# Another order of steps in the second half of a transformer block, on one core

## The chip, the core and the metric

The kernel is one program on one core of a Trainium2 chip. The metric is the device time of one execution in microseconds (us); the median of three runs is the figure that the change is judged by. A core has five engines that run their own instruction lists side by side: TensorE (PE in the rows), VectorE (DVE), ScalarE (ACT), GpSimd (POOL) and SyncE (SP, which here only issues DMAs). They meet by counting semaphores.

## The reference, cut to what matters

```python
x = x + attention(layernorm(x))          # x: 8 batches x 1024 tokens x 256, float32
x = x + ffn(layernorm(x))

# ffn, per token; n = layernorm(x)
gf = global_net(mean over the batch's tokens of n)      # one number for each batch
out = n
for cycle in range(3):
    h = gelu(out @ w1 + b1)      # 256 -> 256
    h = gelu(h @ w2 + b2)        # 256 -> 128
    h = gelu(h @ w3 + b3)        # 128 -> 64
    tf = sigmoid(h @ w4 + b4)    # one number for each token
    coupling = 0.1 + range * ((0.7 * gf + 0.3 * tf) - 0.5) * 2
    out = out + coupling * twist(out)    # twist swaps and negates quarters of the row
```

Since twist applied twice is minus the identity, `out` is always a * n + b * twist(n) with two numbers a, b for each token. So the kernel multiplies n by w1 and by its twisted form once, and each cycle only mixes the two products.

## The kernel before

The first half (attention_phase) ends at about 525 us; the change doesn't touch it. The second half (ffn_phase) treats the 8192 tokens as 16 groups of 512 (NGROUPS, numbered m below; two make a batch). For one group the steps are, with the line that does the main work:

- **stats** (DVE L215 to L221, then the power -1/2 on POOL, L228): mean and 1/sqrt(variance).
- **scale** (DVE L236, four instructions): x0 = normalised tokens.
- **turn** 0, 1 (PE L1272, eight transposes): x0 into PSUM; ACT L1073 copies it (x0T_hi), DVE L1154 makes the rest x0T_lo.
- **product** 0 to 3 (PE L1288 to L1290, six matmuls each): the two products, two chunks of each; ACT L1081 copies each to SBUF (made).
- **global** 0 to 2 (PE L1302, L1307, L1311 with an ACT step behind each, DVE L1160): once in a batch, at its second group.
- Then three cycles c = 0, 1, 2: **spread** c (c = 1, 2; PE L1331: the a and b of the tokens are spread over partitions), **mix** c (DVE L1172, for c = 2 L1169 too, multiply; POOL L1050 adds), **gelu1** c (ACT L1108), **h2** c (PE L1342, ACT L1115), **h3** c (PE L1350 and L1354, ACT L1122), **dot** c (POOL L1057 multiplies by w4, DVE L1180 adds up), **squash** c (ACT L1131 tanh, then small DVE instructions L1222 to L1256 that make the coupling and the new a, b).
- **final** 0 to 3 (DVE L1193, L1201, L1204 each): the result, stored by SP (L1024).

The groups are pipelined. The dictionary PERIODS holds for each engine an order written out by hand: in period n it takes the steps ("kind", ahead, ...) one after the other, each for group m = n + ahead. An engine never changes that order, so a step that waits holds everything behind it on that engine. walk_periods goes through the periods; the first ones and the last ones are written out, the middle is a loop of two turns over four periods (SLOTS). In a period four groups are in flight: one is turned and has its products, and cycles 0, 1 and 2 run on it and the two or three groups before it. In the trace a period is the stretch from one L1272 to the next.

Of the kernel before, what the change touches and what calls it, by code (L numbers as in the profile page):

```python
# [260 lines left out]
def attention_phase(nc, f, x, wqkv, wo, cos_t, sin_t, w, x2):  # L261
# [4 lines left out]
    with ExitStack() as ctx:  # L266
# [606 lines left out]

PERIODS = {
    "tensor": [
        ("product", -1, 0), ("global", -1, 2), ("product", -1, 1), ("spread", -2, 1),
        ("spread", -3, 2), ("product", -1, 2), ("h2", -1, 0), ("product", -1, 3), ("h3", -1, 0),
        ("h2", -2, 1), ("h2", -3, 2), ("turn", 0, 0), ("turn", 0, 1), ("h3", -2, 1),
        ("global", 0, 0), ("h3", -3, 2), ("global", 0, 1),
    ],  # L880
    "scalar": [
        ("product", -1, 3), ("h3", -1, 0), ("h2", -2, 1), ("h2", -3, 2), ("turn", 0, 0),
        ("turn", 0, 1), ("global", 0, 0), ("h3", -2, 1), ("h3", -3, 2), ("global", 0, 1),
        ("squash", -2, 1), ("squash", -1, 0), ("global", 0, 2), ("squash", -3, 2),
        ("product", 0, 0), ("product", 0, 1), ("gelu1", 0, 0), ("h2", 0, 0), ("gelu1", -1, 1),
        ("product", 0, 2), ("gelu1", -2, 2),
    ],
    "vector": [
        ("scale", 0), ("stats", 1), ("turn", 0, 0), ("turn", 0, 1), ("dot", -2, 1), ("dot", -1, 0),
        ("dot", -3, 2), ("squash", -2, 1), ("global", 0, 2), ("squash", -1, 0), ("squash", -3, 2),  # L890
        ("mix", -1, 1), ("mix", -2, 2), ("final", -3, 0), ("final", -3, 1), ("final", -3, 2),
        ("final", -3, 3),
    ],
    "gpsimd": [
        ("dot", -1, 0), ("stats", 1), ("dot", -2, 1), ("dot", -3, 2), ("mix", -1, 1),
        ("mix", -2, 2),
    ],
}
AHEAD = max(step[1] for steps in PERIODS.values() for step in steps)
# [505 lines left out]
```

How the kernel before makes its waits and increments, by code:

```python
def at_least(engine, semaphore, value):  # L39
    if isinstance(value, int) and value <= 0:
        return
    engine.wait_ge(semaphore, value)
# [167 lines left out]
def ffn_moments(dve, f, m, slot, x_tiles):  # L211
    at_least(dve, f.moments_ready, m * G)
    for t in range(G):
        dve.bn_stats(f.stats[:, t, :], x_tiles[t])
    dve.drain()
    for t in range(G):
        dve.bn_aggr(f.moments[slot][:, t, :], f.stats[:, t, :]).then_inc(f.moments_ready, 1)
    dve.wait_ge(f.moments_ready, m * G + G)
    dve.tensor_scalar(f.var_eps[slot][:], f.moments[slot][:, :, 1], EPS, None,
                      ALU.add).then_inc(f.var_ready, 1)
# [2 lines left out]
def ffn_rstd(pool, f, m, slot):  # L225
    pool.wait_ge(f.var_ready, m + 1)
    pool.tensor_tensor(f.rstd[slot][:], f.var_eps[slot][:], f.minus_half[:].to_broadcast([P, G]),
                       ALU.pow).then_inc(f.rstd_ready, 1)
# [2 lines left out]
def ffn_scale(dve, f, m, slot, x0, x_tiles):  # L232
    dve.wait_ge(f.rstd_ready, m + 1)
    for t in range(G):
        dve.tensor_scalar(x0[:, t, :], x_tiles[t], f.moments[slot][:, t, 0:1],
                          f.rstd[slot][:, t:t + 1], ALU.subtract, ALU.mult).then_inc(f.x0_ready, 1)
# [154 lines left out]
        @block.sync  # L392
# [13 lines left out]
            sp.wait_ge(zeroed, 8)
            with nc.allow_non_contiguous_dma(reason="small vectors"):
# [3 lines left out]
            def store_and_load(b, turn, n):  # L413
# [1 line left out]
                for g in range(GROUPS):  # L415
                    sp.wait_ge(x2_ready, b * TILES + G * (g + 1))
                    sp.dma_start(x2_view[b, :, tiles(g), :],
```

## Time and profile before

| | us |
|---|---|
| median of 3 runs | 928.47 |
| the three runs | 931.96, 926.84, 928.47 |
| profiled execution, its span | 926.4 |
| second half in it | 525.7 to 926.4 |
| TensorE busy | 814.3 |
| VectorE busy | 720.2 |
| ScalarE busy | 464.4 |
| GpSimd busy | 363.7 |

The span of the profiled execution is the time from its first to its last instruction. The page gives no figure of its own for what lies around it; the span is 2.1 us under the median of the runs and 0.4 us under the fastest of them. The granted clock is a share of TensorE's full 2.4 GHz; a stretch at 0.5 ran at 1.2 GHz, a stretch between was partly at either level.

### The profile page before, as it was taken

Reading aid. Unit: us, or ns where it says so; the run is one execution under the profiler, and the core shown is the slowest. Engines: PE = TensorE matmul, PEld = TensorE weight load, DVE = VectorE, ACT = ScalarE, POOL = GpSimd, SP = SyncE. Lnnn points to the kernel's source line nnn. Section 1 sums busy time; section 2 is a strip of 40 time slices with the busy share of each in tenths; the row PEclk is TensorE's granted clock in tenths of the full one; section 3 lists DMA queues with packets and bytes.
Section 4 is the critical chain, followed back from the end, with each engine's and each line's share of the span. In section 5 each row is a group of like instructions: output and inputs, shape, how many; then the busy total and the mean of one; then the engine's idle time right before and its main releaser. Section 6 shows DMA issues by size and latency. Waiting matters only on the chain. (4 is left out here: it accounts for less than half of the span.)

```text
span 926.4 us, 15342 instructions
## 1 busy us (share of the span) xinstructions
PE 814.3 (88%) x4368; PEld 644.3 (70%) x4368; DVE 720.2 (78%) x1567; ACT 464.4 (50%) x1020; POOL 363.7 (39%) x377
## 2 busy tenths in 40 slices
PE   4689999998999989999999789988879889999952
PEld 3578788887888868888888557666656666666731
DVE  6779898896998978989978736777777878776575
ACT  2355565554565645565555255444444445444421
POOL 4535644364256434642460014333333334333331
PEclk9889999999999999999999899877897989877865
DMA  6000011101110110011000250000000100000011
GB/s 186 1 1 29 19 46 47 46 1 50 46 36 12 47 49 24 24 47 46 2 0 2 81 192 1 23 24 23 19 28 0 41 27 24 24 24 23 11 35 45
DMA packets 34588, 32.60 MB, mean 35 GB/s; under 512 B 3524, under 2 KB 34244, under 8 KB 34500
## 3 DMA queue, kind: packets, MB, share of 16 engines
q1 hardware_dynamic: 34500, 31.56, 10.7%
q8 instruction: 39, 0.64, 0.3%
q14 instruction: 49, 0.40, 0.1%
HBM read 16.88 MB, written 14.68 MB: 34 GB/s over the span
## 5 line engine op out<-in xcount | busy, mean ns | idle before, releaser
L507 ACT ACTIVATE pT_hi<-bank 128x512 fp32r<-128x512 f32 x192 | 90.9, 492 | 104.6 <-PE bank L843 96.1
L554 ACT ACTIVATE x_all<-scores_ps,neg_max 128x384 f32<-128x384 f32 (+7 forms) x128 | 94.6, 739 | 46.3 <-DVE neg_max L684 42.4
L580 DVE TENSOR_TENSOR pT_lo<-bank,pT_hi 128x512 fp32r<-128x512 f32 x192 | 100.7, 547 | 21.3 <-ACT pT_hi L507 21.3
L684 DVE TENSOR_REDUCE neg_max<-scores_ps 128x1 f32<-128x384 f32 (+7 forms) x128 | 95.3, 749 | 23.9 <-PE scores_ps L816 17.9
L843 PE MATMUL bank<-ident,x_all 128*128 128x128 f32 x576 | 92.7, 279 | 22.3 <-DVE pT_lo L580 17.3
L384 POOL TENSOR_TENSOR rope_a<-x_all,cos_sb 128x384 f32<-128x384 f32 x60 | 61.7, 1028 | 116.7 <-ACT x_all L507 112.6
L1342 PE MATMUL cycle_ps<-h,w_sb 128*128 128x512 f32 x192 | 92.3, 617 | 12.0 <-ACT h L1108 12.0
L843 PEld LDWEIGHTS bank<-ident,x_all 128*128 128x128 f32 x576 | 66.6, 142 | 35.4 <-DVE pT_lo L580 22.3
L1057 POOL TENSOR_TENSOR h_w<-h,w_sb 128x256 f32<-128x256 f32 x48 | 35.6, 742 | 113.1 <-ACT h L1122 113.1
L731 PE MATMUL oT_ps<-pT_hi,v_hi 128*128 128x512 f32 x192 | 77.3, 402 | 0.5 <-DVE oT_lo L580 0.4
L731 PE MATMUL scores_ps<-k_hi,q_hi 128*128 128x512 f32 (+1 forms) x192 | 71.6, 373 | 0.0
L1288 PE MATMUL made_ps<-x0T_hi,w_hi 128*128 128x512 f32 x128 | 68.9, 538 | 2.7 <-DVE x0T_lo L1154 2.7
L1050 POOL TENSOR_TENSOR mixed<-part_b,made 128x1024 f32<-128x1024 f32 x16 | 38.0, 2378 | 81.4 <-DVE part_b L1172 81.4
L1342 PEld LDWEIGHTS cycle_ps<-h,w_sb 128*128 128x128 f32 x192 | 36.0, 196 | 46.6 <-issue 27.4
L732 PE MATMUL oT_ps<-pT_lo,v_hi 128*128 128x512 f32 x192 | 67.0, 349 | 0.0
L497 POOL TENSOR_TENSOR rot<-rope_a,rope_b 128x384 f32<-128x384 f32 x64 | 66.2, 1034 | 1.9 <-DVE rope_a L384 1.8
L733 PE MATMUL oT_ps<-pT_hi,v_lo 128*128 128x512 f32 x192 | 66.9, 348 | 0.0
L483 POOL TENSOR_TENSOR rope_b<-x_all,sin_sb 128x384 f32<-128x384 f32 x64 | 66.4, 1037 | 1.3 <-ACT x_all L507 0.8
L733 PE MATMUL scores_ps<-k_hi,q_lo 128*128 128x512 f32 (+1 forms) x192 | 66.8, 348 | 0.0
L1354 PE MATMUL cycle_ps<-w_sb,h 128*128 128x64 f32 x384 | 66.7, 329 | 0.0
L732 PE MATMUL scores_ps<-k_lo,q_hi 128*128 128x512 f32 (+1 forms) x192 | 66.4, 346 | 0.0
L1354 PEld LDWEIGHTS cycle_ps<-w_sb,h 128*128 128x128 f32 x384 | 59.2, 235 | 7.6 <-issue 3.4
(132 smaller groups left out, 2120.3 us busy)
## 6 DMA issues: line engine op xcount, KB each, us to landing
x_all<-x SPq DMA_DIRECT2D x16, 512.0 KB, 3.6
out<-x_all SPq DMA_DIRECT2D x16, 512.0 KB, 3.0
x<-x_all SPq DMA_DIRECT2D x12, 512.0 KB, 3.0
x_all<-x SPq DMA_DIRECT2D x6, 1024.0 KB, 5.9
x_all<-wqkv SPq DMA_DIRECT2D x1, 512.0 KB, 4.6
sin_sb<-sin_t SPq DMA_DIRECT2D x1, 512.0 KB, 7.0
cos_sb<-cos_t SPq DMA_DIRECT2D x1, 256.0 KB, 5.8
x_all<-wo SPq DMA_DIRECT2D x1, 256.0 KB, 5.9
```

The costliest lines, as they stand in the source:

```text
L483: pool.tensor_tensor(rope_b[:].rearrange("p (c e d) -> p c e d", e=2, d=HALF), qk[:, :, ::-1, :], sin.rearrange("p c (e d) -> p c e d", e= ...
L507: return nc.scalar.activation(out, in_, ACT.Copy)
L554: nc.scalar.activation(probs[u % 2][:, k, 0:keys], scores_ps[k % 2][:, 0:keys], ACT.Exp, bias=neg_max[:, u * G + k:u * G + k + 1], accum_o ...
L580: return dve.tensor_tensor(out, whole, hi.bitcast(F32), ALU.subtract)
L684: dve.tensor_reduce(neg_max[:, u * G + k:u * G + k + 1], scores_ps[k % 2][:, 0:keys], AX_X, ALU.max, negate=True).then_inc(max_ready, 1)
L731: nc.tensor.matmul(out, stationary[0], moving[0], start=first, stop=False)
L732: nc.tensor.matmul(out, stationary[0], moving[1], start=False, stop=False)
L733: return nc.tensor.matmul(out, stationary[1], moving[0], start=False, stop=last)
L843: mm = nc.tensor.transpose(ps[:, k * P:(k + 1) * P], probs[u % 2][:, k, j * P:(j + 1) * P], ident[:])
L1288: nc.tensor.matmul(ps[:], hi, x0T_hi[:, k, :], start=k == 0, stop=False)
L1342: mm = nc.tensor.matmul(cycle_ps[c][:], f.w2_sb[:, k, :], h1[c][:, k, :], start=k == 0, stop=k == DC - 1)
L1354: mm = nc.tensor.matmul(ps[:, t * H3:(t + 1) * H3], h2[c][:, t * P:(t + 1) * P], f.w3_sb[:], start=False, stop=t == G - 1)
```

## The change

Only the four lists of PERIODS are replaced. The steps and what each computes are the same, and so are all waits. Much of the difference in the numbers "ahead" is a renumbering: where all entries of an engine's list are shifted together, its list of instructions stays the same but for the place where the loop closes. What is left, with "T" for the group that is turned in the period, is this.

- PE before: turn T, h3 1, global 0, h3 2, global 1, product 0, global 2, product 1, spread 1, spread 2, product 2, h2 0, product 3, h3 0, h2 1, h2 2. After: turn T, h3 0, global 0, h3 2, global 1, global 2, product 0, spread 1, spread 2, products 1 to 3, h2 0, h2 1, h2 2, h3 1.
- DVE before: turn, dots 1, 0, 2, squashes 1, 0, 2, mix 1, mix 2, finals, scale T+1, stats T+2. After: turn, dots 1, 0, squashes 0, 1, mix 1, mix 2, dot 2, squash 2, finals, scale T+1, stats T+2.
- ACT before: squash 2 ahead of product 0's copy; the copy of product 3 ahead of h3 0. After: squash 2 behind products 0, 1 and gelu1 0; the copy of product 3 behind the turn and h3 0; h2 1 ahead of h2 0.
- POOL before: the power for stats T+2's group between dot 0 and dot 1, ahead of the mixes. After: behind both mixes.

```diff
 PERIODS = {
     "tensor": [
-        ("product", -1, 0), ("global", -1, 2), ("product", -1, 1), ("spread", -2, 1),
-        ("spread", -3, 2), ("product", -1, 2), ("h2", -1, 0), ("product", -1, 3), ("h3", -1, 0),
-        ("h2", -2, 1), ("h2", -3, 2), ("turn", 0, 0), ("turn", 0, 1), ("h3", -2, 1),
-        ("global", 0, 0), ("h3", -3, 2), ("global", 0, 1),
+        ("product", 0, 0), ("spread", -1, 1), ("spread", -2, 2), ("product", 0, 1),
+        ("product", 0, 2), ("product", 0, 3), ("h2", 0, 0), ("h2", -1, 1), ("h2", -2, 2),
+        ("h3", -1, 1), ("turn", 1, 0), ("turn", 1, 1), ("h3", 0, 0), ("global", 1, 0),
+        ("h3", -2, 2), ("global", 1, 1), ("global", 1, 2),
     ],
     "scalar": [
-        ("product", -1, 3), ("h3", -1, 0), ("h2", -2, 1), ("h2", -3, 2), ("turn", 0, 0),
-        ("turn", 0, 1), ("global", 0, 0), ("h3", -2, 1), ("h3", -3, 2), ("global", 0, 1),
-        ("squash", -2, 1), ("squash", -1, 0), ("global", 0, 2), ("squash", -3, 2),
-        ("product", 0, 0), ("product", 0, 1), ("gelu1", 0, 0), ("h2", 0, 0), ("gelu1", -1, 1),
-        ("product", 0, 2), ("gelu1", -2, 2),
+        ("global", 0, 2), ("squash", -1, 0), ("h3", -3, 2), ("product", 0, 0), ("product", 0, 1),
+        ("gelu1", 0, 0), ("squash", -3, 2), ("product", 0, 2), ("gelu1", -1, 1), ("gelu1", -2, 2),
+        ("h2", -1, 1), ("h2", 0, 0), ("h2", -2, 2), ("h3", -1, 1), ("turn", 1, 0), ("turn", 1, 1),
+        ("h3", 0, 0), ("product", 0, 3), ("global", 1, 0), ("global", 1, 1), ("squash", -1, 1),
     ],
     "vector": [
-        ("scale", 0), ("stats", 1), ("turn", 0, 0), ("turn", 0, 1), ("dot", -2, 1), ("dot", -1, 0),
-        ("dot", -3, 2), ("squash", -2, 1), ("global", 0, 2), ("squash", -1, 0), ("squash", -3, 2),
-        ("mix", -1, 1), ("mix", -2, 2), ("final", -3, 0), ("final", -3, 1), ("final", -3, 2),
-        ("final", -3, 3),
+        ("turn", 0, 0), ("turn", 0, 1), ("dot", -2, 1), ("dot", -1, 0), ("global", 0, 2),
+        ("squash", -1, 0), ("squash", -2, 1), ("mix", -1, 1), ("mix", -2, 2), ("dot", -3, 2),
+        ("squash", -3, 2), ("final", -3, 0), ("final", -3, 1), ("final", -3, 2), ("final", -3, 3),
+        ("scale", 1), ("stats", 2),
     ],
     "gpsimd": [
-        ("dot", -1, 0), ("stats", 1), ("dot", -2, 1), ("dot", -3, 2), ("mix", -1, 1),
-        ("mix", -2, 2),
+        ("stats", 2), ("dot", 0, 1), ("dot", 1, 0), ("dot", -1, 2), ("mix", 1, 1), ("mix", 0, 2),
     ],
 }
```

## Rows read from the trace of the kernel before

**Rows 1.** The page: busy time of the engines, and clock in 40 slices

```profile
PE 814.3 (88%) x4368; PEld 644.3 (70%) x4368; DVE 720.2 (78%) x1567; ACT 464.4 (50%) x1020; POOL 363.7 (39%) x377
PEclk9889999999999999999999899877897989877865
```

**Rows 2.** Busy time by stretch, one period each; the columns stand in the first line

```profile
core 0: us, PE busy (x) PEld busy (x) DVE busy (x) ACT busy (x) POOL busy (x), PEclk, DMA share, GB/s
574.21:596.82 22.61, 20.43 (x97) 14.36 (x95) 16.18 (x36) 11.93 (x27) 7.38 (x6) 0.92 0.04 14
...
763.12:784.15 21.03, 19.01 (x95) 13.42 (x95) 17.87 (x45) 11.53 (x26) 8.25 (x6) 1.00 0.07 24
784.15:803.42 19.27, 17.31 (x83) 11.96 (x83) 17.45 (x44) 11.20 (x23) 8.21 (x6) 1.00 0.08 28
803.42:830.44 27.02, 25.08 (x96) 18.36 (x96) 17.87 (x45) 11.46 (x26) 8.23 (x6) 0.75 0.06 20
830.44:855.10 24.66, 22.71 (x90) 16.48 (x91) 17.50 (x43) 11.20 (x24) 8.22 (x6) 0.79 0.10 33
```

**Rows 3.** Waits from 560 to 880 us: total us, times, longest

```profile
PE made_ps L1272 <- DVE x L236: 29.0, 12, 4.9
```

**Rows 4.** Timeline, TensorE, one full-clock period: start, duration, instruction, idle before

```profile
784.15 1.09 PE L1272 MATMUL made_ps<-ident,x 128*128 128x128 f32 x8 [2.02 <-DVE x L236]
...
787.74 0.48 PE L1288 MATMUL made_ps<-x0T_hi,w_hi 128*128 128x512 f32 x1
...
790.63 0.60 PE L1331 MATMUL cycle_ps<-ident,state 128*128 128x128 f32 x4
...
803.42 1.70 PE L1272 MATMUL made_ps<-ident,x 128*128 128x128 f32 x8 [1.96 <-DVE x L236]
```

**Rows 5.** Timeline, VectorE and GpSimd from the mixes to the scaling

```profile
791.30 1.23 DVE L1172 TENSOR_TENSOR part_b<-cycle_ps,made 128x1024 f32<-128x1024 f32 x1
...
792.61 2.37 POOL L1050 TENSOR_TENSOR mixed<-part_b,made 128x1024 f32<-128x1024 f32 x1 [3.44 <-DVE part_b L1172]
...
794.71 0.55 DVE L1193 SCALAR_TENSOR_TENSOR y_part<-x,state,x_all 128x256 f32<-128x256 f32 x1
794.93 2.57 POOL L1050 TENSOR_TENSOR mixed<-part_b,part_a 128x1024 f32<-128x1024 f32 x1
...
795.29 2.35 DVE L1201 SCALAR_TENSOR_TENSOR x_all<-x,state,y_part 128x128 f32<-128x128 f32 x1
...
797.57 0.34 DVE L1204 SCALAR_TENSOR_TENSOR x_all<-x,minus_b,y_part 128x128 f32<-128x128 f32 x1
...
801.99 1.38 DVE L236 TENSOR_SCALAR x<-x_all,f_moments,f_rstd 128x256 f32<-128x256 f32 x4
```

**Rows 6.** Timeline, first and last instruction of squash 2, and gelu1 0

```profile
790.43 0.28 DVE L1228 TENSOR_SCALAR coupling<-token_tanh,range_token,base_coupling 128x4 f32<-128x4 f32 x1
...
791.22 0.17 DVE L1256 TENSOR_SCALAR minus_b<-state 128x4 f32<-128x4 f32 x1
...
791.46 1.34 ACT L1108 ACTIVATE h<-made,b_sb 128x512 f32<-128x512 f32 x2
```

**Rows 7.** Timeline, small instructions of VectorE and GpSimd side by side

```profile
572.63 0.73 POOL L1057 TENSOR_TENSOR h_w<-h,w_sb 128x256 f32<-128x256 f32 x1 [2.37 <-ACT h L1122]
572.86 0.52 DVE L221 TENSOR_SCALAR f_var_eps<-f_moments 128x4 f32<-128x4 f32 x1
...
786.15 1.02 POOL L228 TENSOR_TENSOR f_rstd<-f_var_eps,minus_half 128x4 f32<-128x4 f32 x1 [4.85 <-DVE f_var_eps L221]
...
799.90 0.81 DVE L1204 SCALAR_TENSOR_TENSOR x_all<-x,minus_b,y_part 128x128 f32<-128x128 f32 x1
```

**Rows 8.** Timeline, product 1 and spread 1 of a low-clock period

```profile
839.14 0.63 PE L1288 MATMUL made_ps<-x0T_hi,w_hi 128*128 128x512 f32 x1
...
841.52 0.60 PE L1331 MATMUL cycle_ps<-ident,state 128*128 128x128 f32 x4
```

**Rows 9.** Timeline, VectorE where the loop closes

```profile
693.49 1.38 DVE L236 TENSOR_SCALAR x<-x_all,f_moments,f_rstd 128x256 f32 x4 [2.91 <-issue]
```

**Rows 10.** Timeline, spread 1 of the last group, at low clock

```profile
883.16 1.12 PE L1331 MATMUL cycle_ps<-ident,state 128*128 128x128 f32 x4 [2.63 <-DVE state L1222]
```

## The prediction

> **What bounds the kernel now.** I read the page's busy times and clock first, then busy time by period, then the waits, then the timeline of one clean period. The page says TensorE is busy for 88% and VectorE for 78% [rows 1], so TensorE looks like the bound. In the second half the periods say otherwise: at full clock a period is 19.27 us, of which TensorE works 17.31 and VectorE 17.45 [rows 2]. TensorE stops once in each period, ahead of turn, until VectorE has scaled x0: 12 times, 29.0 us [rows 3]. So the bound is a ring through both engines. TensorE: turn, two h3, products 0 and 1, spread 1, that is 790.63 - 784.15 = 6.48 us. Then VectorE: three multiplies of the mixes, four finals, scale; the next turn comes 803.42 - 790.63 = 12.79 us after spread 1 [rows 4]. The two make the 19.27.
>
> Within those 12.79 us lies a second thing to see. A final should take a fraction of a microsecond per instruction; the first L1201 takes 2.35 us and ends where GpSimd's second mix ends (794.93 + 2.57 = 797.50; the next starts at 797.57) [rows 5]. VectorE is held while GpSimd works. It isn't only the wide ones: L221 on 128x4 takes 0.52 us and ends with the dot that runs beside it (573.38 and 573.36), and L1204, else 0.34, takes 0.81 [rows 5, 7]. And they take turns: y_part waits out the first mix, the second mix starts behind it, and L1201 waits for that [rows 5].
>
> The third is the clock. Eight of the twelve periods from 574.21 to 855.10 stand below 0.95; the first and the last of them are shown. A low one costs 5 to 6 us: 24.66 against 19.27 without the global steps, 27.02 against 21.03 with them [rows 2].
>
> **The change, part by part.** Much is renumbering and costs nothing. Four things move.
>
> *Product 1 leaves the way to spread 1.* Two products take 790.63 - 787.74 = 2.89 us at full clock, so one is worth 1.45 us [rows 4]; at low clock product 1 took 841.52 - 839.14 = 2.38 us [rows 8]. h3 0 takes h3 1's place behind the turn, same size. Its chain (ACT, dot, reduce, tanh, coupling) has h3 2 and product 0 as cover, some 3 us; I price it at nothing, and if the cover is short by its reduce it costs 0.4. Gain: 1.45 us, or 2.38.
>
> *Dot 2 and squash 2 move behind the mixes.* Before, they ran while VectorE waited for spread 1, and cost nothing. After, squash 2 stands ahead of the finals. Its tanh stands on ACT behind product 1's copy and gelu1 0 (1.34 us [rows 6]); product 1 is now made behind the spreads, so gelu1 0 ends about 4.8 us behind spread 1 (spreads 1.25, product 1.45, copy 0.6, gelu 1.34, hand-overs). By then GpSimd's second mix runs: in the old trace it covers 4.3 to 6.9 us behind spread 1 [rows 4, 5], and the new order leaves that alone. So squash 2's first instruction waits for the end of that mix, exactly where the first final waited before. What was inside that wait is then outside it: squash 2 (791.22 + 0.17 - 790.43 = 0.96 us [rows 6]) and the first y_part (0.5 us [rows 5]). Cost: 1.46 us in each period. Bounds: 0.5, if squash 2 gets through during the mix, and 1.9, if the reduce (0.42 us) is late too.
>
> *GpSimd's power for the next group moves behind the mixes.* It takes 1.02 us [rows 7] and before ran right behind its own statistics, where VectorE had nothing of this kind to do. Now it is ready and queued when the second mix ends, so by the turn-taking of rows 5 it gets in between two of squash 2's instructions, and the next one waits. No row shows the power beside an instruction of this kind. Bounds: nothing, and 1.02 us. I take 1.02: of the GpSimd instructions beside which such a VectorE instruction stood, dot and mix, both held it to their end. The Trainium skill (SBUF — State Buffer, Who interferes with whom) has the rule: a VectorE instruction with two SBUF inputs contends with a GpSimd instruction that reads SBUF, and the loser blocks for the whole instruction. By it the term is 1.02, by the rows alone anything between the two bounds; none here decides.
>
> *The global steps.* Global 2 no longer has product 0 between itself and global 1, so TensorE waits for one ACT step: 0 to 0.8 us in every second period, I take 0.4. Global 0 is unmoved.
>
> The dot in the finals is now dot 1 and not dot 0: the hold of 0.47 us (0.81 - 0.34) stays, priced at no change (0.5 either way). At low clock the spreads now fall partly into the slow stretch: a spread of 1.12 us against 0.60 [rows 4, 10], 0.5 us more ahead of the first multiply. SP's queue holds only stores, later by as much as the finals are, and no one waits for them but the end. The loop of VectorE now closes behind stats and not ahead of scale: its 2.9 us [rows 9] will be partly hidden by h3, a gain up to 0.9, but ACT's closing now lies between squash 1 and squash 0, on the ring, at up to 2 us once. I take 0.
>
> **The sum.** Full clock: -1.45 + 1.46 + 1.02 = +1.03 us. Low clock: -2.38 + 1.46 + 1.02 + 0.5 = +0.60 us. With the old clock pattern 4 x 1.03 + 8 x 0.60 + 6 x 0.4 = +11.3 us. In the drain product 1 leaves the last group's way too (-2.4 us), and finals 13 and 14 come later by 1.5 but have slack, as the last group's h3 is what is late next. Net +8.9: 926.4 + 8.9 = 935.3 us as a span. The median of the runs is 2.1 us over the profiled span, so 937.4; I say **938**.
>
> **Rivals.** (1) *The clock falls in the full periods too.* From the end of h2 to product 0 TensorE has only thin work: before, the gap of 2.0 us, turn and two h3; after, a third h3, and a gap of 12.79 + 1.46 + 1.02 = 15.3 less the 12.79 - 1.96 + 1.45 = 12.3 us of work, 3.0 us. Four periods at 5.4 to 6.0 us more: +22, 960. Half of that is as likely as all, 948. For it: every low stretch before began in or behind such thin work. Against: global periods, the thinner ones, were low less often than the others (two or three of six against five of six).
> (2) *The power doesn't hold VectorE.* Then 12 x 1.02 = 12.2 us less: 925.
>
> (3) *Squash 2's small instructions are not held, nor is anything by the power* (the other side). They then run under the second mix, and 12 x (0.96 + 1.02) = 23.8 us go: 914. It decides by when the tanh arrives: if more than 1 us ahead of the mix's end and unheld. For it: instructions on 128x4 may find a gap. Against: L221, of that size, was held.
> (4) *It changes nothing*, because most is renumbering and what is left trades wait for wait: 928.
>
> **Chances.** Forecast (932 to 945) 0.48; (1) 0.15; (2) 0.14; (3) 0.15; (4) 0.08. The point is the forecast's. The range takes in (2), half of (1) and part of (3): 918 to 955. A measurement here can tell about 0.5% (4.6 us) from no change. Faster: (3) and a little of (2), 0.17. Same: (2), (4) and the forecast's lower edge, 0.25. Slower: the rest, 0.58.
>
> **What would show it.** Right: spread 1 comes about 5.1 us behind turn at full clock; L1228 or the TENSOR_TENSOR L1245 behind it takes over 1 us and ends with a mix or the power; the first L1201 takes 0.35; the wait of L1272 for L236 grows towards 3 us. Wrong: squash 2's instructions at 0.16 to 0.29 us while L1050 runs, or the turns under 19 us apart; or a clock that is higher than before, which none of my terms has.

## The result, and the profile after

| | before | after |
|---|---|---|
| median of the runs | 928.32 us (926.84 to 931.96) | 951.86 us (948.97 to 954.51) |
| span of the profiled execution | 926.4 us | 949.9 us |
| mean granted clock of TensorE | in the second half between 0.75 and 1.00 by period | 0.75 to 0.79 in eleven periods of twelve |

The ratio is 1.025, with a 95% interval from 1.020 to 1.029. The change makes the kernel slower, by 23.5 us. The forecast was slower by 9.7 us (938): the sign was right, and 951.86 lies in the stated range (918 to 955), but the loss is more than twice the forecast one.

The page of after (busy time of the engines; the clock in 40 slices), to be read beside [rows 1]:

```profile
span 949.9 us, 15349 instructions
PE 838.9 (88%) x4368; PEld 670.2 (71%) x4368; DVE 710.1 (75%) x1567; ACT 466.7 (49%) x1020; POOL 360.8 (38%) x377
PEclk9889999999999999999999799777777777777765
```

As many instructions as before on each engine. VectorE, GpSimd and ScalarE do the same work in about the same time (VectorE even 10 us less); TensorE needs 838.9 us where it needed 814.3. The last third of the clock line stands at 7, but for the drain at its end; before, 9s and 8s stood among the 7s. That is where the time went, and the busy time by period says it with numbers. After, four of the twelve (columns as in [rows 2]):

```profile
core 0: us, PE busy (x) PEld busy (x) DVE busy (x) ACT busy (x) POOL busy (x), PEclk, DMA share, GB/s
575.68:598.14 22.46, 20.27 (x97) 14.73 (x96) 15.90 (x36) 11.96 (x27) 8.73 (x7) 0.92 0.05 16
...
673.72:700.91 27.19, 24.37 (x95) 18.44 (x96) 17.85 (x45) 11.76 (x26) 7.90 (x6) 0.75 0.06 19
700.91:725.04 24.13, 21.56 (x83) 15.74 (x84) 17.06 (x44) 11.20 (x23) 8.01 (x6) 0.78 0.06 22
...
853.68:877.36 23.68, 21.93 (x84) 16.11 (x84) 16.80 (x43) 11.09 (x23) 7.92 (x6) 0.78 0.07 23
```

All twelve, one turn to the next, in us with the granted clock in brackets (the odd ones hold the global steps; the twelfth of before ends at its turn, 854.30):

| | 1 | 2 | 3 | 4 | 5 | 6 | 7 | 8 | 9 | 10 | 11 | 12 |
|---|---|---|---|---|---|---|---|---|---|---|---|---|
| before | 22.61 (.92) | 22.71 (.85) | 27.37 (.75) | 24.20 (.79) | 23.90 (.99) | 24.06 (.80) | 21.34 (1.00) | 22.72 (.85) | 21.03 (1.00) | 19.27 (1.00) | 27.02 (.75) | 23.86 (.79) |
| after | 22.46 (.92) | 24.23 (.78) | 27.27 (.75) | 24.08 (.78) | 27.19 (.75) | 24.13 (.78) | 27.15 (.75) | 24.00 (.78) | 27.17 (.75) | 23.48 (.79) | 26.84 (.75) | 23.68 (.78) |

The reader is to see two things. Where the clock is the same in both (1, 3, 4, 6, 11, 12), the periods differ by -0.18 to +0.07 us, -0.7 together. Where it isn't (2, 5, 7, 8, 9, 10), after takes 1.3 to 6.1 us more, 22.2 together. One of these holds a second difference: in before, VectorE's loop closes ahead of the scaling in period 5 [rows 9], and the turn behind it waits 4.91 us where its neighbours wait 2.34, so 2.6 us of the 23.90 are this closing. In after the closing stands behind stats, and TensorE, at half clock, doesn't notice it (turn to spread 1 takes 9.24 us there as in the other periods without global steps). First the line of before, then two of after:

```profile
695.00 1.96 PE L1272 MATMUL made_ps<-ident,x 128*128 128x128 f32 x8 [4.91 <-DVE x L236]
...
700.91 1.96 PE L1270 MATMUL made_ps<-ident,x 128*128 128x128 f32 x8 [2.47 <-DVE x L236]
...
705.56 1.29 DVE L1152 TENSOR_TENSOR x0T_lo<-made_ps,x0T_hi 128x512 fp32r<-128x512 f32 x2 [2.81 <-issue]
```

So the lower clock costs some 24.8 us and the closing gives back 2.6. The rest of the 23.5 lies ahead of the first of these turns (575.68 against 574.21, +1.5) and in the drain behind the last (72.5 against 72.1, +0.4).

What VectorE and GpSimd do from the second mix to the first final, after, in a low-clock period:

```profile
714.70 2.39 POOL L1048 TENSOR_TENSOR mixed<-part_b,part_a 128x1024 f32<-128x1024 f32 x1
715.09 0.28 ACT L1129 ACTIVATE token_tanh<-logit,b_half 128x4 f32<-128x4 f32 x1
...
715.50 1.62 DVE L1226 TENSOR_SCALAR coupling<-token_tanh,range_token,base_coupling 128x4 f32<-128x4 f32 x1 [0.74 <-ACT token_tanh L1129]
...
717.04 1.03 POOL L228 TENSOR_TENSOR f_rstd<-f_var_eps,minus_half 128x4 f32<-128x4 f32 x1
717.25 0.17 DVE L1243 TENSOR_TENSOR scaled<-state,coupling 128x8 f32<-128x8 f32 x1
717.54 0.17 DVE L1249 TENSOR_TENSOR state<-state,scaled 128x4 f32<-128x4 f32 x1
...
718.24 0.48 DVE L1191 SCALAR_TENSOR_TENSOR y_part<-x,state,x_all 128x256 f32<-128x256 f32 x1 [0.25 <-DVE minus_b L1254]
718.76 0.35 DVE L1199 SCALAR_TENSOR_TENSOR x_all<-x,state,y_part 128x128 f32 x1
```

The lines are two lower than before (L1226 is the old L1228, L1199 the old L1201). The coupling waits for the second mix and ends with it (717.12, the mix at 717.09), as forecast; the first L1199 is down from 2.35 us to 0.35. But beside the power the small instructions take 0.17 us: it doesn't hold them.

TensorE in the same period and the next, after:

```profile
721.37 1.10 PE L1352 MATMUL cycle_ps<-w_sb,h 128*128 128x64 f32 x8
725.04 1.96 PE L1270 MATMUL made_ps<-ident,x 128*128 128x128 f32 x8 [2.57 <-DVE x L236]
...
727.45 1.97 PE L1352 MATMUL cycle_ps<-w_sb,h 128*128 128x64 f32 x8
...
737.31 0.83 PE L1329 MATMUL cycle_ps<-ident,state 128*128 128x128 f32 x4
```

h3 1 still has the full clock (1.10 us), then comes a pause of 2.57 us, and turn takes 1.96 where a full-clock one takes 1.09 [rows 4]: the clock is at its half level, 1.2 GHz, when the pause ends. It comes back at spread 1, 12 us later. So it goes in all: of the twelve turns with such a pause ahead of them eleven take 1.88 to 1.97 us and the last 1.68. Before, six of twelve took 1.09 us, and the clock then fell behind them or not at all. The waits from 560 to 900 us show that the pause itself has hardly changed (29.0 us in [rows 3]):

```profile
PE made_ps L1270 <- DVE x L236: 27.3, 12, 2.6
```

### The profile page after: what moved, and what is told of

Same layout as the page of the kernel before. It is cut to its first block and busy times, and to the rows that moved or that the text cites. A ratio compares the mean times of both kernels' runs of the same rounds, so it can differ in the third digit from the quotient of the medians.

```text
span 949.9 us, 15349 instructions
## 1 busy us (share of the span) xinstructions
PE 838.9 (88%) x4368; PEld 670.2 (71%) x4368; DVE 710.1 (75%) x1567; ACT 466.7 (49%) x1020; POOL 360.8 (38%) x377
## 5 line engine op out<-in xcount | busy, mean ns | idle before, releaser
L1340 PE MATMUL cycle_ps<-h,w_sb 128*128 128x512 f32 x192 | 89.8, 617 | 11.1 <-ACT h L1106 11.1
L1352 PE MATMUL cycle_ps<-w_sb,h 128*128 128x64 f32 x384 | 73.8, 354 | 0.0
L1079 ACT ACTIVATE made<-made_ps 128x512 f32<-128x512 f32 x64 | 37.8, 590 | 72.5 <-PE made_ps L1288 72.5
L1352 PEld LDWEIGHTS cycle_ps<-w_sb,h 128*128 128x128 f32 x384 | 65.9, 259 | 8.4 <-issue 5.4
L1286 PE MATMUL made_ps<-x0T_hi,w_hi 128*128 128x512 f32 x128 | 62.1, 485 | 2.6 <-DVE x0T_lo L1152 1.5
```

The lines of the kernel that those rows point to most:

```text
L1340: mm = nc.tensor.matmul(cycle_ps[c][:], f.w2_sb[:, k, :], h1[c][:, k, :], start=k == 0, stop=k == DC - 1)
L1352: mm = nc.tensor.matmul(ps[:, t * H3:(t + 1) * H3], h2[c][:, t * P:(t + 1) * P], f.w3_sb[:], start=False, stop=t == G - 1)
```

## The experiments

Each was compared with the kernel before on the same chip. Its median differed by chip (937.3 beside the runs e1, e2, e4 and e5, 930.5 beside e3, e6, e7 and e8, 935.2 beside e9 to e12), so the ratios are what is to be compared. The time is the median, and the ratio to the kernel before has its 95% interval; after itself stands at 1.025. The two theories: the moved steps themselves cost the time (the sum of the forecast), or the clock of TensorE does (its first rival).

**The power back ahead of the mixes.** After, with the power between GpSimd's first two dots as before the change (dot 1 stays ahead of dot 0):

```diff
     "gpsimd": [
-        ("stats", 2), ("dot", 0, 1), ("dot", 1, 0), ("dot", -1, 2), ("mix", 1, 1), ("mix", 0, 2),
+        ("dot", -2, 1), ("stats", 1), ("dot", -1, 0), ("dot", -3, 2), ("mix", -1, 1),
+        ("mix", -2, 2),
```

> The changed kernel with one part undone: GpSimd takes the power (L228) behind dot 1, ahead of the mixes, as before the change. If the power holds squash 2's instructions for 1.02 us in every period, as the prediction had it, about 12 us come back: 940. If it holds nothing but the first y_part (in the changed kernel the small instructions ran at 0.16 to 0.17 us beside it, and y_part started 0.2 us late), 2 to 3 us: 949 to 950, and the first y_part starts without the 0.25 us of idle time. Neither says anything of the clock, which should stay at 0.75 to 0.79 in every period.

Measured: 953.57 us, 1.018 (1.012 to 1.025); span 951.6, clock 0.885. The twelve periods take 300.7 us, after 301.7. VectorE behind the second mix, in this kernel:

```profile
744.76 1.69 DVE L1227 TENSOR_SCALAR coupling<-token_tanh,range_token,base_coupling 128x4 f32<-128x4 f32 x1 [0.66 <-ACT token_tanh L1130]
746.58 0.17 DVE L1244 TENSOR_TENSOR scaled<-state,coupling 128x8 f32<-128x8 f32 x1
...
747.48 0.48 DVE L1192 SCALAR_TENSOR_TENSOR y_part<-x,state,x_all 128x256 f32<-128x256 f32 x1 [0.25 <-DVE minus_b L1255]
```

The same durations, and the same 0.25 us ahead of y_part, without the power. So the power's term, 1.02 us in each period, was nothing. It is these rows that show it: the two ratios, 1.018 and 1.025, differ by 0.7%, and their intervals would leave room for anything from nothing to 1.4%.

**Squash 2 back ahead of the mixes.** After, with dot 2 and squash 2 ahead of the mixes again on VectorE, and squash 2 right behind h3 2 on ScalarE:

```diff
     "scalar": [
-        ("global", 0, 2), ("squash", -1, 0), ("h3", -3, 2), ("product", 0, 0), ("product", 0, 1),
-        ("gelu1", 0, 0), ("squash", -3, 2), ("product", 0, 2), ...
+        ("global", 0, 2), ("squash", -1, 0), ("h3", -3, 2), ("squash", -3, 2), ("product", 0, 0),
+        ("product", 0, 1), ("gelu1", 0, 0), ("product", 0, 2), ...
     "vector": [
-        ("squash", -1, 0), ("squash", -2, 1), ("mix", -1, 1), ("mix", -2, 2), ("dot", -3, 2),
-        ("squash", -3, 2), ("final", -3, 0), ...
+        ("squash", -1, 0), ("squash", -2, 1), ("dot", -3, 2), ("squash", -3, 2), ("mix", -1, 1),
+        ("mix", -2, 2), ("final", -3, 0), ...
```

> The changed kernel with one part undone: dot 2 and squash 2 stand ahead of the mixes again on VectorE, and squash 2 right behind h3 2 on ScalarE. If the loss is VectorE's, that squash 2 and the first y_part now follow the second mix, 1.5 us come back in each of 13 periods: 932, with the clock still at 0.75 to 0.79. If the loss is the clock's and the clock falls because TensorE's pause ahead of turn and the thin work around it are longer, the pause shortens from 2.5 to about 1 us and the clock is full in some periods: 905 to 925. If the clock falls because of h3 1 ahead of the pause and h3 0 behind it, it stays low: 932.

Measured: 905.93 us, 0.968 (0.961 to 0.974); span 904.4, clock 0.932. One step put back is worth some 50 us against after (0.968 and 1.025), and the kernel is faster than before. Two periods of it (the second with global steps), the wait ahead of turn from 560 to 900 us, and the stretch where the power stands beside a final:

```profile
728.70:748.86 20.16, 17.81 (x83) 12.01 (x84) 18.00 (x44) 11.09 (x23) 8.63 (x7) 1.00 0.10 33
748.86:773.88 25.02, 24.67 (x96) 18.94 (x96) 17.97 (x45) 11.21 (x25) 7.45 (x5) 0.73 0.05 16
```

```profile
PE made_ps L1270 <- DVE x L236: 9.0, 9, 1.7
```

```profile
720.25 2.56 POOL L1048 TENSOR_TENSOR mixed<-part_b,part_a 128x1024 f32<-128x1024 f32 x1
...
720.61 2.34 DVE L1199 SCALAR_TENSOR_TENSOR x_all<-x,state,y_part 128x128 f32 x1
...
722.77 1.06 POOL L228 TENSOR_TENSOR f_rstd<-f_var_eps,minus_half 128x4 f32<-128x4 f32 x1
...
722.88 0.34 DVE L1202 SCALAR_TENSOR_TENSOR x_all<-x,minus_b,y_part 128x128 f32 x1
```

The non-global periods of the loop stand at 1.00 with one exception (0.85), the pause is down from 27.3 to 9.0 us, and turn takes 1.09 us again. The forecast's 1.46 us a period for squash 2 would be 17.5 us, and the pause is shorter by 18.3; that the other 30 or so are the clock is read from the periods at 1.00, not tested by itself. L1202 has two operands from SBUF and runs in 0.34 us beside the power; L1199, beside the mix, takes 2.34.

**The pause filled, in both kernels.** Twelve matmuls of 128x384 into a part of a PSUM bank that nothing reads, ahead of turn's wait; first after, then before:

```diff
                         c, = rest
+                        if c == 0:
+                            for _ in range(12):
+                                nc.tensor.matmul(global_ps[:, P:], f.w1_hi[0][:, 0, 0:P],
+                                                 f.w1_hi[0][:].rearrange("p c n -> p (c n)")[:, 0:3 * P],
+                                                 start=True, stop=True)
                         pe.wait_ge(f.x0_ready, m * G + G)
```

> The changed kernel with 12 added matmuls (128x384, into unused columns of global_ps, nothing reads them) on TensorE ahead of the wait of turn, some 2 us of dense work at full clock in the pause of 2.5 us. If the clock is what costs (all periods at 0.75 to 0.79 against four full ones before), the clock rises in most periods and the time falls below the kernel before: periods of 20.2 and 21.9 us against 24.1 and 27.2, so 12 x 4.6 = 55 us less, 897; half of that if only half of the periods stay up. If the clock is not the cause, 952 or a little more.

> The kernel before with the same 12 added matmuls ahead of the wait of turn, into its pause of 2.0 to 2.35 us. At full clock its periods are 19.3 and 21.0 us, 20.2 on average against 23.4: 38 us less if the clock then stays up throughout, 890. The difference to the changed kernel with the same filling is what the moved steps cost without the clock: by the changed kernel's trace (14.9 us from spread 1 to turn against 13.2, less 1.45 for product 1) 0 to 4 us over the whole. If thin work behind the turn alone brings the clock down, part stays: 905 to 928.

Measured: after with filling 915.60 us, 0.978 (0.972 to 0.984); before with filling 914.72 us, 0.977 (0.971 to 0.983). TensorE of after with filling around turn, and its twelve periods as one stretch:

```profile
715.03 1.10 PE L1357 MATMUL cycle_ps<-w_sb,h 128*128 128x64 f32 x8
715.95 2.33 PE L1268 MATMUL global_ps<-w_hi 128*128 128x384 f32 x12
718.63 1.09 PE L1275 MATMUL made_ps<-ident,x 128*128 128x128 f32 x8 [0.34 <-DVE x L236]
...
719.96 1.10 PE L1357 MATMUL cycle_ps<-w_sb,h 128*128 128x64 f32 x8
```

```profile
581.33:845.00 263.67, 254.84 (x1213) 188.68 (x1212) 206.16 (x513) 135.07 (x294) 96.02 (x72) 0.95 0.07 24
```

And after itself, the same twelve:

```profile
575.68:877.36 301.68, 272.32 (x1071) 202.21 (x1070) 206.83 (x513) 137.79 (x295) 96.18 (x73) 0.78 0.06 21
```

Twelve matmuls more in each period, and 38.0 us less in all; TensorE is busy for 17.5 us less, with more to do. No step has moved; turn takes 1.09 us, and the clock is 0.95. The same stretch of before with filling:

```profile
581.01:840.47 259.46, 254.72 (x1214) 186.76 (x1212) 210.69 (x513) 135.62 (x294) 96.75 (x71) 0.95 0.07 24
```

So with the clock kept up in both, what is left between the two orders is 0.9 us by the medians, which the intervals don't tell from nothing, and 4.2 us by the twelve periods. These are the runs that decide: of the change's 23.5 us all or nearly all is the clock's. They also give the full-clock period that after itself doesn't have: 5.08 us from turn to spread 1 and 14.99 to the next turn, 20.07 in all (turn at 650.14), beside 6.47 and 13.29, 19.76, in before with filling (turn at 645.08). The three other pairs of such periods differ by 0.4 to 0.8 us. At full clock the new order costs 0.3 to 0.8 us a period, where at half clock it costs nothing.

**Half the filling** (six instead of twelve, in after):

> The changed kernel with half of e4's filling: 6 dense matmuls, about 1 us of the pause of 2.5. If the clock goes by how much of the stretch is thin or idle, half the filling (thin plus pause from 7.5 to 6.5 us) lifts the clock in part of the periods: between 916 and 952, about 925 to 935. If any dense work near the pause is enough, the same as with 12: 916. If the pause has to be filled to its end, 952.

Measured: 913.84 us, 0.978 (0.970 to 0.986), the same as with twelve.

**Thin filling.** The same twelve matmuls in after, with 2 columns instead of 384:

```diff
+                                nc.tensor.matmul(global_ps[:, P:P + 2], f.w1_hi[0][:, 0, 0:P],
+                                                 f.w1_hi[0][:, 1, 0:2], start=True, stop=True)
```

> A control to the filling with dense matmuls: the changed kernel with 12 added matmuls of two columns (128x2 in place of 128x384) ahead of the wait of turn. The engine is then occupied through most of the pause, but with weight loads and almost no columns. If the clock goes by dense work, nothing changes: 950 to 955 with all periods at 0.75 to 0.79. If it goes by whether TensorE has instructions at all, the clock rises as with the dense ones: 915.

Measured: 965.14 us, 1.039 (1.036 to 1.042). TensorE around turn:

```profile
734.66 1.10 PE L1356 MATMUL cycle_ps<-w_sb,h 128*128 128x64 f32 x8
735.57 1.48 PE L1268 MATMUL global_ps<-w_hi 128*128 128x2 f32 x12
738.32 1.96 PE L1274 MATMUL made_ps<-ident,x 128*128 128x128 f32 x8 [1.27 <-DVE x L236]
```

The pause is halved, 2.5 to 1.3 us, and the clock falls all the same; the periods are those of after (24.1 and 27.2 us). The 13 us more lie ahead of the twelve periods (their first turn comes at 585.57 against 575.68; the period ahead of it stands at 0.77 and takes 22.5 us, in after at 1.00 and 17.1) and in the first of them (25.5 against 22.5). So shortening the idle time is not enough: cut from 2.5 to 1.3 us by instructions of few columns, it loses the clock as before; with six or twelve wide ones in the same place the clock stays up in most periods.

**h3 0 back behind product 3.** After, with this step of TensorE where it was. h2 0 goes with it, ahead of product 3, and ScalarE takes h2 0, the copy of product 3 and h3 0 earlier to match (not shown here), so it is more than one step:

```diff
     "tensor": [
         ("product", 0, 0), ("spread", -1, 1), ("spread", -2, 2), ("product", 0, 1),
-        ("product", 0, 2), ("product", 0, 3), ("h2", 0, 0), ("h2", -1, 1), ("h2", -2, 2),
-        ("h3", -1, 1), ("turn", 1, 0), ("turn", 1, 1), ("h3", 0, 0), ("global", 1, 0),
+        ("product", 0, 2), ("h2", 0, 0), ("product", 0, 3), ("h3", 0, 0), ("h2", -1, 1),
+        ("h2", -2, 2), ("h3", -1, 1), ("turn", 1, 0), ("turn", 1, 1), ("global", 1, 0),
```

> The changed kernel with h3 0 back behind product 3, in the dense stretch, on TensorE and ScalarE; squash 2 stays late. The way from turn to spread 1 loses one h3 (1.35 us, 2.4 at low clock), the pause stays near 2.5 or grows by up to 1.4. If three h3 around the pause are what brings the clock down in every period, full periods come back: 890 to 915. If the late squash 2 with its pause is enough, the clock stays at 0.75 to 0.80 and only the h3 is saved: 952 - 12 x 2.4 = 923.

Measured: 920.33 us, 0.988 (0.986 to 0.991); span 919.2, clock 0.934. Two periods:

```profile
742.47:761.65 19.18, 17.80 (x86) 11.94 (x85) 16.46 (x44) 10.98 (x23) 7.86 (x6) 1.00 0.08 26
761.65:784.36 22.71, 20.63 (x97) 14.55 (x97) 17.51 (x44) 11.54 (x26) 7.81 (x6) 0.92 0.06 19
```

No turn waits for VectorE any more: with one h3 less between turn and the spreads VectorE starts earlier, and with one more ahead of turn TensorE arrives later. The coupling is still held by the second mix (up to 1.65 us in the loop), so the late squash 2 is still there, and costs nothing that shows.

**Squash 2 late in the kernel before.** The counter-test to the second experiment:

```diff
     "scalar": [
-        ("squash", -2, 1), ("squash", -1, 0), ("global", 0, 2), ("squash", -3, 2),
-        ("product", 0, 0), ("product", 0, 1), ("gelu1", 0, 0), ("h2", 0, 0), ...
+        ("squash", -2, 1), ("squash", -1, 0), ("global", 0, 2),
+        ("product", 0, 0), ("product", 0, 1), ("gelu1", 0, 0), ("squash", -3, 2), ("h2", 0, 0), ...
     "vector": [
-        ("dot", -3, 2), ("squash", -2, 1), ("global", 0, 2), ("squash", -1, 0), ("squash", -3, 2),
-        ("mix", -1, 1), ("mix", -2, 2), ("final", -3, 0), ...
+        ("squash", -2, 1), ("global", 0, 2), ("squash", -1, 0), ("mix", -1, 1), ("mix", -2, 2),
+        ("dot", -3, 2), ("squash", -3, 2), ("final", -3, 0), ...
```

> The kernel before with the other move alone: dot 2 and squash 2 behind the mixes on VectorE, squash 2 behind gelu1 0 on ScalarE. The finals come 1.5 to 1.7 us later in each period, so without any effect on the clock it is 12 x 1.6 = 19 us slower than the kernel before. If the longer pause (then about 3.9 us) alone brings the clock down in every period, the four full ones go too: 22 us more, 41 us slower in all (970 to 978). If only the thin work behind the turn decides, the pattern stays and it is 19 us.

Measured: 962.35 us, 1.035 (1.033 to 1.038); span 956.2, clock 0.909. One pause and what follows:

```profile
761.21 1.09 PE L1272 MATMUL made_ps<-ident,x 128*128 128x128 f32 x8 [3.92 <-DVE x L236]
762.23 0.58 PE L1350 MATMUL cycle_ps<-b_parts,ones_r 33*128 33x256 f32 x1
762.74 1.54 PE L1354 MATMUL cycle_ps<-w_sb,h 128*128 128x64 f32 x6
```

The pause grows from 2.34 to 3.92 us. That 1.58 is the forecast's term for squash 2 (1.46), alone. The twelve waits grow from 29.0 to 47.2 us, 18 of the 32 lost; the rest is the clock, which falls behind turn in this one (the first six of L1354 take 1.54 us here, all eight 1.97; at full clock all eight take 1.10) and stands at 0.72 to 0.86 in all periods but the first. This part of the change hurts by itself, without the other. In after product 1 is made between spread 1 and the next turn, so its 1.45 us fill as much of the pause as squash 2 adds, which is why after's pause is as long as before's.

**h3 1 ahead of turn in the kernel before.**

```diff
     "tensor": [
-        ("h2", -2, 1), ("h2", -3, 2), ("turn", 0, 0), ("turn", 0, 1), ("h3", -2, 1),
+        ("h2", -2, 1), ("h2", -3, 2), ("h3", -2, 1), ("turn", 0, 0), ("turn", 0, 1),
     "scalar": [
-        ("turn", 0, 1), ("global", 0, 0), ("h3", -2, 1), ("h3", -3, 2), ("global", 0, 1),
+        ("h3", -2, 1), ("turn", 0, 0), ("turn", 0, 1), ("global", 0, 0), ("h3", -3, 2), ("global", 0, 1),
```

> The kernel before with one move of the change alone: h3 1 stands ahead of the turn on TensorE and ScalarE, so it runs in TensorE's pause. Both theories of the clock agree that the pause shrinks from 2.0 to 2.35 us to about 0.7 to 1.0; the way from turn to spread 1 is 1.35 us shorter (2.4 at low clock), worth 12 x 1.35 to 2.4 = 16 to 29 us on 928 to 937. If the sum of pause and thin work (h3, pause, turn, h3) decides over the clock, it is 4.7 us against 5.7 and more periods are full: another 10 to 20 us. If it is only the place of the thin work ahead of the pause that brings the clock down, most periods are low and the gain is eaten: 925 to 945.

Measured: 914.73 us, 0.983 (0.981 to 0.985); span 913.5, clock 0.931. The pause is 0.6 to 1.1 us, and the non-global periods stand at 1.00 (18.9 to 19.5 us), with one exception: where VectorE's loop closes the pause is 3.50 us, turn takes 1.96, and the period behind it stands at 0.82 (21.98 us). The periods with global steps stay at 0.83 to 0.92. After moves h3 1 as well, but sends h3 0 behind turn in its place, and squash 2 behind the mixes, and the pause is back.

**Both parts back, and filling on top.** After with h3 0 and squash 2 both in their old places; that with six filling matmuls; and after with squash 2 alone back and six filling matmuls:

> Both undone in the changed kernel: squash 2 ahead of the mixes (as in e2, 46 us less than the changed kernel) and h3 0 back in the dense stretch (as in e7, 32 us less). e7 has no pause ahead of turn any more, so TensorE's own work bounds its periods, and an earlier squash 2 can't shorten them. If thin work plus pause decides over the clock, e9 has what e7 has, no pause, and comes out near it or a little lower: 900 to 920. If the two gains added up it would be 875.

> e9 with 6 dense matmuls (128x384, about 1 us) ahead of the wait of turn. There is hardly a pause to fill, so they cost up to 1 us in each of 16 periods; they split the thin work (h3 1, turn, h3 2) in two. If that keeps the clock up in the global periods too, which e7 had at 0.86 to 0.93, it wins 2 to 3 us in each of six: 895 to 915. If not, it is 10 to 16 us slower than e9.

> e2 (the changed kernel with squash 2 back ahead of the mixes, 906 us beside 937 for the kernel before) with 6 dense matmuls ahead of the wait of turn, where it has a pause of 0.2 to 1.7 us. Its global periods were still low (0.73 to 0.92, 21.6 to 25 us against 21 at full clock). If the filling keeps them up, 3 us in each of six periods less: 888 to 900. If the filling pushes turn later and the thin work behind it brings the clock down anyway, 905 to 915.

Measured: 917.58 us, 0.982 (0.974 to 0.990); 927.08 us, 0.992 (0.988 to 0.996); 903.77 us, 0.967 (0.959 to 0.975). The two repairs don't add up: with h3 0 back TensorE has no pause left, so there is nothing for squash 2's place to shorten, and a filling has to be paid: 9.5 us in all, and 20.3 us for a full-clock period where it was 19.2. Where a pause of 0.2 to 1.7 us is left, the filling costs nothing, though it gains nothing that these runs can tell from 905.93 either: the periods with global steps take 21.6 to 23.1 us with it and 20.8 to 25.0 without. This last kernel and the one without filling are 3.3 and 3.2% under before, the fastest found.

## Why the prediction was right or wrong

**The bound, a ring through turn and the finals: right.** Turn waits for the scaling twelve times in after too, 27.3 us. Spread 1 to the next turn takes 14.9 us in the loop's non-global periods, against 13.2 before in the loop: 1.7 more; forecast were 1.46, 0.5 for the spreads at half clock, and the power's 1.02, which is treated below.

**Product 1 off the way to spread 1: right, a little too much at half clock.** With the global steps turn to spread 1 is 12.27 us (725.04 to 737.31), 14.24 before, 1.97 less; the forecast for these periods was 2.38 less 0.4 for global 2, 1.98. Without them it is 1.6 to 1.9 less where 2.38 were forecast: in the old order the clock comes back inside product 1 (from 656.14 to 657.92 in one such period, 1.78 us). At full clock it is 1.4 (6.48 and 5.08 us), forecast 1.45.

**Squash 2 and the first y_part behind the second mix: right, with its mechanism.** The coupling takes 1.62 us and ends with the mix, L1199 takes 0.35 for 2.35, and the move alone lengthens the pause by 1.58 us in the kernel before. Rival 3, that they run under the mix, is out. Rival 4, that nothing changes, held for the order at half clock and not for the time.

**The power holds VectorE: wrong.** This is the first term that was mis-sized: 1.02 us a period, 12.2 in all, measured nothing (the same durations with it and without). I had two bounds and no row, and took the upper because dot and mix both hold. The Trainium skill (SBUF — State Buffer, Who interferes with whom) has the loser blocked for the whole of the other's instruction; the runs don't bear that out for this one: L1202 with two SBUF operands takes 0.34 us in the middle of a power of 1.06. Rival 2 was right on the mechanism, and I gave it 0.14; its time, 925, was not, for the clock's sake.

**Global 2 (0.4): right. The spreads at half clock (0.5): too much.** TensorE waits for global 2's ScalarE step seven times, 2.4 us in all, 0.34 each. From spread 1 to the next turn the half-clock periods take 1.7 to 1.8 us more than before, which leaves 0.2 to 0.35 for the spreads. In the six periods with an unchanged clock the sum was to be +0.6 to +1.0 each, and they came out at -0.1. The power's 1.02 is what parts them; the smaller errors of product 1 and the spreads nearly cancel.

**The loop closing of VectorE (0): missed.** I had a gain of up to 0.9 us and took none; it is 2.6, once.

**The clock: the step that failed.** The sum was made "with the old clock pattern", 4 full periods and 8 low ones, and that was the largest assumption in it. As a rival it was priced about right, 5.4 to 6.0 us for a full-clock period that falls: periods 7 and 9 lost 5.8 and 6.1, period 10 4.2, period 5 3.3 (5.9 without the loop closing), and the two at 0.85 lost 1.5 and 1.3. That makes the 22.2 us. The 5.4 was a misreading: the window of 24.66 us ends at 855.10, 0.8 us behind the next turn, and turn to turn the difference is 23.86 - 19.27 = 4.6. Rival 1's 960, less the power, is 948; the runs say 952. I gave it 0.15, with half of it another part of the range. What I held against it, that the global periods, the thinner ones, were low less often, went by the pattern of a single run. What I should have weighed is that eight of before's twelve periods were low or partly so already. The kernel before moves by itself, too: on one chip it took 927.4 us at a mean clock of 0.923 and 940.5 at 0.904.

The expected signs went as follows: the second and third came as described, the first (spread 1 5.1 us behind turn at full clock) only in the run with filling, since after has no such period (5.08 us), and the wait of L1272 didn't grow towards 3 us (2.6 at most), as the power's 1.02 was missing from it. A lower clock was not among my signs at all. Drain: forecast -2.4, measured +0.4 (spread 1 of the last group comes 0.7 us sooner behind its turn, what follows takes 1.2 us longer), and the start of the phase +1.5 where I had nothing; neither was followed further.

Put together: forecast +11.3 for the periods, -2.4 for the drain; measured -0.7 for the order in the periods that can be compared, -2.6 for the loop closing, +24.8 for the clock, +0.4 and +1.5 for the ends.

**What is shown and what isn't.** Shown: the loss is TensorE's clock (filling takes it away, all but 0.9 to 4.2 us, in a kernel that is otherwise the same). Shown: in the new order, undoing either of the two parts, squash 2's place or h3 0's (with h2 0), brings full-clock periods back. In the old order squash 2's late place alone is enough to lower the clock in nearly all periods, so h3 0's place is not needed for a loss. Not shown: which property of the stretch the chip reacts to. After has h3 1, the pause, turn and two h3 in a row, 7.5 us at full clock by an estimate from their rows, where before had the pause, turn and two h3, 5.7 us. An added h3 can't be the whole cause: the old order with the late squash 2 has none and loses as well, with a pause of 3.9 us and 7.5 us for the whole stretch. A longer stretch of pause and few columns fits both, but the clock falls at other places in them (in the pause in after, mostly behind turn in the other), and no run changes the length of the stretch and nothing else. That the remaining low-clock periods of the better kernels (0.73 to 0.93, nearly all with global steps) have the same cause is argued, not tried.

The Trainium skill (TensorE: Matmul & The Clock Gate, HAM oscillation — how this bites in real kernels) tells of a kernel that loses the clock anew in each of its steps, because each step's work is short against its wait. This case agrees in that, eleven turns in a row start at half clock, but not in the reason: here a wait of 2.5 us stands beside some 21.6 us of TensorE's work in a period.

## What to carry to other kernels

Where TensorE stops once in every period and works on few columns around the stop, list the periods with their granted clock before anything else, and treat a mixed pattern (here 0.75 to 1.00) as an edge: forecast a change first by whether it adds to the thin stretch or takes from it, and only then by its waits. A pause that can't be scheduled away can be tested, and here cured, in one edit: a few wide matmuls into PSUM space that nothing reads, ahead of the wait. It costs next to nothing while it fits into the pause, and about its own length where there is none (1.1 us in a full-clock period). Moving an h3 (1.4 us) ahead of the wait did the same with real work in the kernel before (0.983), as long as nothing lengthened the pause again.

## What the runs showed of the hardware

- **More work, less time.** Six matmuls of 128x384 in a pause of 2.5 us brought the kernel from 1.025 of before's time to 0.978, and twelve likewise.
- **Matmuls of few columns don't keep the clock up.** Twelve of 128x2 took 1.48 us of the pause, turn was still at 1.96 us, and the time rose to 1.039.
- **GpSimd's instructions don't all hold VectorE.** A TENSOR_SCALAR on 128x4 takes 0.28 us alone, 1.62 to 1.95 us beside a mix (128x1024), and 0.5 to 0.8 beside a dot (128x256; 0.17 alone for the one that took 0.5). The power on 128x4, 1.03 us long, held nothing: 0.16 to 0.17 us for the small instructions beside it, 0.34 for L1202.
